# A state-space layer with its feed-forward block on one core: in the scan, a tile's increments go in front of the later logits, and its seed copy in front of the exponentials

## The reference, cut to what matters

```
delta = softplus(dt_r @ W_dt + b_dt)
A     = -exp(A_log)
def step(h, (d_t, B_t, C_t, u_t)):
    dA  = exp(d_t[:, :, None] * A)
    h   = h * dA + (d_t * u_t)[:, :, None] * B_t[:, None, :]
    y_t = einsum('bdn,bn->bd', h, C_t)
```

## Time and profile before

| What | us |
|---|---|
| median of 3 runs | 6156.26 (6154.0 to 6156.75) |
| the profiled execution's own time | 6154.45 |
| span of the profile, first to last instruction | 6152.6 |
| first scan starts, last scan starts | 928.4, 5473.6 |
| VectorE busy in the scans | 4499.2 |

### The profile page before, as it was taken

The page is one execution under the profiler, slowest core; times in us unless marked ns, Lnnn a source line. Parts: engine busy times, 40 slices in busy tenths (PEclk is TensorE's granted clock), DMA queues, the critical chain, the costliest instruction groups (busy, mean ns, idle before and its releaser), DMA issues. The chain is left out here.

```text
span 6152.6 us, 147986 instructions
## 1 busy us (share of the span) xinstructions
PE 5492.5 (89%) x37915; PEld 2419.3 (39%) x38396; DVE 5559.3 (90%) x3491; ACT 3328.5 (54%) x7982; POOL 2612.2 (42%) x6848
## 2 busy tenths in 40 slices
PE   2889839999999999999999999999999999979998
PEld 1333313333333333333333333333333333336666
DVE  8799959999999999999999999999999999974343
ACT  1667636566565565565555555655656656631111
POOL 4244444444444444444444444444444444420000
PEclk9988869999999999999999999999999999989999
DMA  4888872222222222222222222222222222233331
GB/s 148 280 295 301 291 242 54 54 52 52 53 53 52 53 53 52 53 53 52 53 53 51 53 53 51 53 53 51 54 53 51 54 53 51 54 95 99 103 109 65
DMA packets 1105505, 547.14 MB, mean 89 GB/s; under 512 B 753744, under 2 KB 1015056, under 8 KB 1105056
## 3 DMA queue, kind: packets, MB, share of 16 engines
q1 hardware_dynamic: 1093776, 533.89, 32.4%
q10 hardware_dynamic: 11664, 12.52, 0.6%
HBM read 296.83 MB, written 249.82 MB: 89 GB/s over the span
## 5 line engine op out<-in xcount | busy, mean ns | idle before, releaser
L971 DVE TENSOR_TENSOR_SCAN s_h<-s_decay,s_ubank 128x1024 f32<-128x1024 f32 x2048 | 4499.2, 2267 | 81.6 <-ACT s_ubank L940 80.4
L923 ACT ACTIVATE s_decay<-s_abank 128x512 f32<-128x512 f32 x4096 | 2234.9, 604 | 1763.5 <-PE s_abank L861 1763.5
L846 PE MATMUL s_ybank<-s_h,s_window 128*8 128x256 f32 x16416 | 1948.2, 602 | 1.9 <-DVE s_h L971 1.9
L861 PE MATMUL s_abank<-s_x,s_a 128*128 128x256 bf16 x8192 | 1425.4, 276 | 310.9 <-DMA s_x<-scratch_u_rows 73.6
L1008 POOL TENSOR_TENSOR s_carry<-s_decay,s_h 128x64 f32<-128x64 f32 x2032 | 882.3, 434 | 1781.3 <-ACT s_decay L923 1030.3
L891 PE MATMUL s_ubank<-s_x,s_w 128*128 128x256 bf16 x8192 | 1234.7, 273 | 38.3 <-DVE s_h L971 4.0
L861 PEld LDWEIGHTS s_abank<-s_x,s_a 128*128 128x128 bf16 x8192 | 591.8, 97 | 1270.8 <-ACT s_decay L923 707.3
L891 PEld LDWEIGHTS s_ubank<-s_x,s_w 128*128 128x128 bf16 x8192 | 735.9, 98 | 288.3 <-DVE s_h L971 183.0
L1012 POOL TENSOR_TENSOR s_seed<-s_carry,s_first 128x64 f32<-128x64 f32 x2048 | 657.9, 321 | 164.4 <-ACT s_first L929 4.0
L846 PEld LDWEIGHTS s_ybank<-s_h,s_window 128*8 128x8 f32 x16416 | 377.2, 97 | 838.6 <-issue 835.5
L1014 POOL TENSOR_TENSOR s_decay<-s_none 128x64 f32<-128x64 f32 x2048 | 619.9, 303 | 0.0
(11 more groups left out here) (123 smaller groups left out, 3197.8 us busy)
## 6 DMA issues: line engine op xcount, KB each, us to landing
s_x<-scratch_u_rows SPq DMA_DIRECT2D x4096, 32.0 KB
scratch_u_rows<-p_u_turn SPq DMA_DIRECT2D x90, 1024.0 KB, 6.4
scratch_delta_rows<-p_dparts SPq DMA_DIRECT2D x136, 512.0 KB, 5.7
s_x<-scratch_delta_rows SPq DMA_DIRECT2D x1024, 64.0 KB, 2.7
scratch_y<-s_y SPq DMA_DIRECT2D x1036, 16.0 KB
scratch_sz<-p_sz SPq DMA_DIRECT2D x16, 1024.0 KB, 5.8
scratch_u<-p_u SPq DMA_DIRECT2D x16, 1024.0 KB, 7.3
s_w<-scratch_b_rows SPq DMA_DIRECT2D x256, 64.0 KB, 2.4
```

The lines of the kernel that those rows point to most:

```text
L846: last = nc.tensor.matmul(y_bank[32 * ct:32 * ct + WIN, 1 - x, :], window[:, of, (at + t) * WIN:(at + t + 1) * WIN], H[:, 1 - x, :, t], st ...
L861: last = nc.tensor.matmul(a_bank[:, b, jj], a_w[:, half, j, :], x1[:, g, :, half, j, s * T:(s + 1) * T], start=True, stop=True)
L923: nc.scalar.activation(dst.rearrange("p x q t -> p q x t"), a_bank[:, b].rearrange("p j r (x t) -> p (j r) x t", x=2), ACT.Exp).then_inc(e ...
L971: nc.vector.tensor_tensor_scan(H[:, x, PT * p:PT * p + PT, :].rearrange("p q t -> p (q t)"), decay[:, x * (1 + c % 2), p].rearrange("p q t ...
```

## The change

It moves one block on TensorE and one on ScalarE. In each tile TensorE now has: firsts (k = 0, 4), wait for scan k - 2, I(k), L(k + 5), C(k) if k is odd. ScalarE has: wait for I(k) and the seed, S(k), E(k + 5), then Y and F. No instruction, wait, shape or buffer is added or removed, and the other three engines' lists are the same.

```diff
--- TensorE, chunk()
-                    if k + LEAD < GROUPS:
-                        logits(it, f, c, k + LEAD)
-                    elif not last_one:
-                        logits(it + (c + 1) // 4, f + 1, (c + 1) % 4, k + LEAD - GROUPS)
                     pe.wait_ge(scan_done, n + 7)
                     for b in range(2):
                         ...
                     last.then_inc(u_ready, 1)
+                    if k + LEAD < GROUPS:
+                        logits(it, f, c, k + LEAD)
+                    elif not last_one:
+                        logits(it + (c + 1) // 4, f + 1, (c + 1) % 4, k + LEAD - GROUPS)
                     if p in CONTRACT:
                         contract(f, s, x, CONTRACT[p])
--- ScalarE, chunk()
                     n, x = f * TILES + k, k // BLOCKS
+                    act.wait_ge(u_ready, n + 17)
+                    act.wait_ge(carried, n * 3 + 2)
+                    nc.scalar.activation(u_bank[:, k % 2, :, 0], seed[:, k % CPS, :], ACT.Identity).then_inc(seeded, 1)
                     if k + LEAD < GROUPS:
                         exps(f, c, k + LEAD)
                     elif not last_one:
                         exps(f + 1, (c + 1) % 4, k + LEAD - GROUPS)
-                    act.wait_ge(u_ready, n + 17)
-                    act.wait_ge(carried, n * 3 + 2)
-                    nc.scalar.activation(u_bank[:, k % 2, :, 0], seed[:, k % CPS, :], ACT.Identity).then_inc(seeded, 1)
```

## The result

| What | before | changed |
|---|---|---|
| median, us (4 runs each) | 6155.13 (6153.64 to 6156.75) | 6069.59 (6068.24 to 6070.3) |
| span of the profile | 6152.6 | 6067.2 |
| first to last scan start | 4545.2 | 4460.4 |

The ratio is 0.986, with a 95% interval of 0.9848 to 0.9872. The kernel is 85.5 us faster. The spans differ by 85.4: 0.9 because the first scan starts earlier, 84.8 between the first and the last scan's start, and 0.3 against it in the rest.

The account below looks back on a forecast made before the run. It took VectorE's scans at 2.193 us a step as the bound, with late scans at every second chunk's tile 4. Gaps of 56.1 plus 0.8 at the start gave 56.9 off 6156.26: 6099.4 us, range 6093 to 6135.

Parts of the forecast that it names:

- I(7) of two chunks before: TensorE, x2 rows: logits L(9) start 11.73 us after this I(7), which stays tied to VectorE, so the landing costs nothing or up to 0.22.
- the floor: Scan stage: VectorE's own rate, 2047 steps at 2.193 us, 4489.1 us; no reordering gets below it.
- all gaps together 56.1: Scan stage: 4545.2 us from first to last scan start less 4489.1 at VectorE's own rate; all of it to be won.
- The 0.8 for the earlier start: Start of the scan stage: I(0) takes the place of L(5), so the first scan starts 0.8 us earlier, between nothing and 1.1.
- the overlap of 0.07: VectorE: neighbouring queued scans overlap by 0.07 us, counted on top of the slacks of 0.20, 0.21 and 0.28.
- The walk: One chunk of the new order stepped through with measured durations: every seed copy ends in time, the chunk 17.54 us long.
- S(3)'s 0.28: Tile 3: seed copy S(3), behind E(7) and GpSimd's chain, ends at 6.26 against 6.54, a slack of 0.28 us.
- Rival 1: Tiles 0, 3 or 4: part of the gaps stays, 0.15 a chunk giving back 38 us, 6138 (6105 to 6143); chance 0.13.
- rival 3: Tile 3: seed late behind E(7) and GpSimd's chain, a gap of 0.83 a chunk, slower at 6311 us; chance 0.12.
- Rival 2: TensorE is the bound, so nothing comes of the change: 6144 to 6168 us, middle 6156; chance 0.08.

Follow-up runs that it names:

- both first increments at odd tiles: Kernel before, old order, with the next chunk's first increments moved from tile 4 to 5 and the other pair from tile 0 to 1: 6068.25 us, ratio 0.9854.
- the short contraction: Kernel before, old order, with two of the four token steps of each group's contraction left out: 6138.56 us, ratio 0.9969.
- the run with two operations: Changed kernel with GpSimd's clear and one more operation of that size in front of the seed of tile 3: 6126.68 us, ratio 0.9952.
- The two halves alone: Kernel before with only TensorE's reordering, 6547.08 us, or only ScalarE's, 6878.21 us; one run each.
- the two versions with the same loop: Changed kernel with VectorE instead of GpSimd zeroing the second half of x1, 6056.9 us, or the first half, before all else, 6055.15 us.
- the run with one clear in front: Changed kernel with GpSimd's clear in front of the seed instead of behind it, ScalarE waiting for both: 6070.79 us, ratio 0.9862.

## Why the prediction was wrong

**What bounds the kernel.** Right: VectorE, with gaps at every second tile 4, begun by the x2 rows and drawn out by L(9) and E(9). Moving `firsts` by one tile removes the wait and the gap. (Its "I(7) of two chunks before" counts from the chunk whose rows land; seen from the late tile 4 it is the chunk before. The times used are the right ones.)

**The step that failed.** "Inside a run of 16 scans the time from start to start is 2.193 us, always, so there VectorE has its next scan ready." It was not so: 2.193 is a mean over 15 steps of which seven were long (three of 2.217 and four of 2.204, one of these right behind the late tile 4), 0.22 us in all; the same 0.015 a step is in the sixteenth, so that 30.7 us of waiting went into the floor. The runs put 2.178 in its place, in the old order (both first increments at odd tiles, and the short contraction inside its runs) as in the new. The term "all gaps together 56.1" was therefore 4545.2 - 2047 x 2.178 = 86.8, and the changed kernel took 84.8 of it. The 0.8 for the earlier start was 0.9. With the right step the prediction's own sum gives 6156.26 - (86.8 + 0.8) = 6068.7, against 6069.59.

**What led to it.** I treated the overlap of 0.07 between neighbouring scans as slack, and took a row without idle time for an engine that waits for nothing. The seed copy of tile 0 ended 0.03 ahead of its scan in the earlier trace rows (3024.85 + 0.23 = 3025.08, with the scan due at 3016.34 + 4 x 2.193 = 3025.11); that this equals the 0.04 at the scan which visibly waited was the sign, and I took 0.03 as "ahead". A second sign stood in the earlier trace rows: a mean length of 2267 ns with a median of 2261 and a maximum of 2289. A late scan is itself shown 0.026 longer, 2.29 in the single scans above where the others have 2.26, and (2267 - 2261) / 26 says that about a quarter of all scans were late; it was four in sixteen.

**The walk.** Right, within 0.1 at each step, and so was its slack where a run tested it: S(3)'s 0.28 is 0.31 by the run with two operations. The walk closed with TensorE waiting for VectorE at each odd tile, which the trace shows. The two halves alone, walked with the same durations, came out at 6500 and 6900 against 6547 and 6878. The prediction did not walk the order of before. With the same durations it gives I(7) -4.24, C(7) -3.70, L(5) -1.64, E(5) 0.42 later at -1.22, and S(0) from -0.25 to -0.02, where it must end at -0.04: no slack, and the hidden wait in sight.

**The rivals.** Rival 1 (gaps stay) and rival 3 (tile 3) did not happen; rival 3's mechanism is real and begins where the walk put it. Rival 2 asked whether TensorE is the bound. It isn't: half of its contraction taken away gave only 19 us of 6158, and no step inside those runs came below 2.178. But it was nearer than the prediction thought. In before its weight loads wait 0.35 for a scan ahead of I(3) and I(7), its matmuls only 0.07 (3010.78 + 0.88 to 3011.73), and behind I(7) its list reaches tile 0 too late by the hidden 0.04:

```profile
3010.78 0.88 PE L861 MATMUL s_abank<-s_x,s_a 128*128 128x256 bf16 x4
3011.72 0.33 PEld L891 LDWEIGHTS s_ubank<-s_x,s_w 128*128 128x128 bf16 x4 [0.34 <-DVE s_h L971]
3011.73 0.61 PE L891 MATMUL s_ubank<-s_x,s_w 128*128 128x256 bf16 x4
```

**Two rules beside the trace.** The Trainium skill ("VectorE: DVE Perf Modes", section "The DRAIN you can't avoid") says that the next operation does not start until the pipe has emptied, unless it is one that isn't held. Taken without the exception, as the prediction tried it, the rule is further off than it seemed: 2.26 shown against a step of 2.178. The Trainium skill ("Perfetto Trace Analysis", section "Identifying the Most-Contended Engine") says that for VectorE the occupancy is a fair measure of how close one is to the roofline. Here it was 98.9% in the stage, and 1.9% of the stage could be gained; the measurement decides.

**What stays open.** Why the step behind a late scan is 2.204 rather than 2.178, though its seed is there 0.57 early. The late scan's own length in the rows is longer by just this, 2.287 against 2.261, in each run that has late scans; no run shows why.

## What to carry to other kernels

Compute the step of a saturated engine from single starts, sorted by their place in the loop, and take the smallest that repeats; a mean over a run without idle time can hide waits, since neighbouring instructions overlap in the rows. A wait shows instead in the distance between the releaser's end and the start: if it is that of a hand-off (0.03 here), the instruction was late, whatever the idle column says. A mean length above the median is worth a look too: here it counted the late scans. Where two engines hand each other work in program order, a reordering of one list alone can lose what both together win; walk the loop with measured durations, which here was right to 0.1 us, and walk the old order first.

## What the runs showed of the hardware

- Scans of 128 x 1024 fp32 follow each other every 2.178 us when released in time, with 2.26 to 2.30 shown as the length of each. The shown length is no price: its median was 2.30 in the profile of the changed kernel and 2.26 in those of the two versions with the same loop, at the same step.
- A scan released late costs its lateness and 0.026 us more at the next; it is shown 2.287 long instead of 2.261. One whose seed copy ends 0.04 us before it starts costs nothing (the run with one clear in front).
- From the end of a seed copy to the start of the scan that waits for it: 0.03. From the end of GpSimd's seed to the seed copy that waits: 0.03. From the end of the increments, as modelled, to the copy: 0.12.
